# Cross-attention with layer norm in three-pass float32: queries and output tiles as half-row matmuls that share TensorE's rows

## The reference

```python
Q = (x @ w_q.T)      # 16 heads of 32
K = (ctx @ w_k.T); V = (ctx @ w_v.T)
attn = softmax(Q K^T / sqrt(32))      # over 64 keys, per head
o = (attn V) @ w_o.T + b_o
y = layernorm(o + x) * gamma + beta
```

## Time and profile before

| what | value |
|---|---|
| median of 3 runs | 613.66 us (613.42 to 614.11) |
| profiled execution, its own time | 615.86 us |
| its span in the trace | 614.1 us |
| PE busy | 585.9 us (95%) |
| DVE, ACT, POOL busy | 473.2, 444.1, 480.9 us (77%, 72%, 78%) |
| mean granted clock of PE | 0.981 |

### The profile page before, as it was taken

The page is one execution under the profiler, slowest core; times in us unless marked ns, Lnnn a source line. Parts: engine busy times, 40 slices in busy tenths (PEclk is TensorE's granted clock), DMA queues, the critical chain, the costliest instruction groups (busy, mean ns, idle before and its releaser), DMA issues.

```text
span 614.1 us, 8719 instructions
## 1 busy us (share of the span) xinstructions
PE 585.9 (95%) x2602; PEld 425.7 (69%) x2602; DVE 473.2 (77%) x864; ACT 444.1 (72%) x794; POOL 480.9 (78%) x334
## 2 busy tenths in 40 slices
PE   8968789999999999999999999999999999999874
PEld 7745567777777777777777777777777777777553
DVE  7356678888888888888888888888888888888536
ACT  7437777787777877778777787777877778766620
POOL 4336759888898888988889888898888988868740
PEclk9979999999999999999999999999999999999779
DMA  8333413333343334333343233432344321222232
GB/s 311 101 98 85 132 45 98 87 94 113 113 117 86 93 112 118 114 87 91 114 121 115 83 91 115 118 111 86 90 120 117 112 86 50 74 73 74 71 103 86
DMA packets 84223, 63.05 MB, mean 103 GB/s; under 512 B 56752, under 2 KB 56752, under 8 KB 84176
## 3 DMA queue, kind: packets, MB, share of 16 engines
q1 hardware_dynamic: 81936, 62.23, 34.4%
q10 hardware_dynamic: 2240, 0.26, 0.3%
HBM read 39.39 MB, written 16.78 MB: 91 GB/s over the span
## 4 chain that ended last, share of the span: by engine, by line
PE 91%; ACT 2%; DVE 2%; POOL 1%; issue 1%; ACTq 1%; DMA 0%; SPq 0%; DVEq 0%
PE ps_o L280 30%; PE ps_q L280 29%; PE ps_c L280 15%; PE ps_s L334 9%; PE ps_s L344 5%; PE ps_s L280 2%; ACTq L165 1%; ACT probs L476 1%; POOL p_lo L682 1%; PE ps_c L287 1%; DVE z L630 0%; ACT p_hi L409 0%; DMA max_rows<-max_turned 0%; DVE c_raw L605 0%; ACT inverse L483 0%
## 5 line engine op out<-in xcount | busy, mean ns | idle before, releaser
L682 POOL TENSOR_TENSOR p_lo<-probs,p_hi 128x1024 fp32r<-128x1024 f32 x64 | 153.9, 2404 | 53.9 <-ACT p_hi L409 53.9
L576 DVE STREAM_TRANSPOSE turned<-ps_s 128x1024 f32<-128x1024 f32 x64 | 80.0, 1250 | 46.3 <-PE ps_s L334 46.3
L280 PE MATMUL ps_q<-x_hi,wq_lo 128*128 128x512 f32 x256 | 108.7, 425 | 0.0
L280 PE MATMUL ps_o<-wo_hi,c_lo 128*128 128x512 f32 x256 | 104.4, 408 | 2.3 <-POOL c_lo L697 2.3
L470 ACT ACTIVATE inverse<-ps_c 64x512 f32<-64x512 f32 x64 | 38.2, 597 | 89.8 <-PE ps_c L280 89.8
L280 PE MATMUL ps_o<-wo_hi,c_hi 128*128 128x512 f32 x256 | 103.0, 402 | 0.0
L280 PE MATMUL ps_o<-wo_lo,c_hi 128*128 128x512 f32 x256 | 102.9, 402 | 0.0
L280 PE MATMUL ps_q<-x_hi,wq_hi 128*128 128x512 f32 x256 | 102.0, 399 | 0.0
L280 PE MATMUL ps_q<-x_lo,wq_hi 128*128 128x512 f32 x256 | 101.9, 398 | 0.0
L690 POOL TENSOR_TENSOR y<-y,gamma_row 128x512 f32<-128x512 f32 x60 | 77.6, 1293 | 20.4 <-ACT y L512 20.4
L672 POOL TENSOR_TENSOR x_lo<-xT_raw,x_hi 128x512 fp32r<-128x512 f32 x60 | 78.0, 1301 | 18.0 <-ACT x_hi L409 18.0
(11 more groups left out here) (92 smaller groups left out, 1139.4 us busy)
## 6 DMA issues: line engine op xcount, KB each, us to landing
xT_raw<-in_xT SPq DMA_DIRECT2D x64, 256.0 KB, 3.3
x_raw<-in_x SPq DMA_DIRECT2D x64, 256.0 KB, 2.7
out<-y SPq DMA_DIRECT2D x64, 256.0 KB, 2.2
max_rows<-max_turned SPq DMA_DIRECT2D x128, 16.0 KB
ctx_raw<-in_ctxT SPq DMA_DIRECT2D x4, 256.0 KB, 4.2
wk_raw<-in_wkT SPq DMA_DIRECT2D x4, 256.0 KB, 4.4
wq_raw<-in_wqT SPq DMA_DIRECT2D x4, 256.0 KB, 5.9
wv_raw<-in_wvT SPq DMA_DIRECT2D x4, 256.0 KB, 6.8
```

What stands on the lines that cost most here:

```text
L280: mm = nc.tensor.matmul(dst, lhs, rhs, start=(first and n == 0), stop=(last and n == len(passes) - 1))
L576: nc.vector.transpose(turned[:, :], ps_s[:, 2 * s:2 * s + 2, :].rearrange("p b r -> p (b r)")).then_inc(turned_done, 1)
L682: nc.gpsimd.tensor_tensor(p_lo[:, :, :], probs[:, :, :], p_hi[:, :, :].bitcast(fp32), ALU.subtract).then_inc(p_lo_done, 1)
```

## The change

`project_both(n, i, second)` takes the place of `project_queries` and `project_output` in the 56 turns (t = 7 to 62) that have both. Each matmul over 128 rows becomes two over 64 rows. In the first half the queries use rows 0 to 63 and the output tile rows 64 to 127, alternating; then `score(t)` follows; in the second half they change sides, after a wait until the first half's sums have arrived (`first_halves_done`). `combine_values` does the same with the two pairs of heads, in a first and a second part with `subtract_max` and the next tile's bias between them, and comes one turn later. The maxima are read over 64 rows of `select` and `max_rows` (zeros added), and the bias over 64 rows of `signs`. Outputs lag by 7 turns instead of 6, so there is one turn more in all; x is split 5 ahead instead of 6. Buffers are placed anew to make room. The orders on ACT, DVE, POOL and SP are rewritten.

```diff
-    OUT_LAG = 6
-    SPLIT_AHEAD = 6
+    OUT_LAG = 7
+    SPLIT_AHEAD = 5
     LAST = 4
     WARM = 10
...
+                    pe.wait_ge(bias_filled, 16)
                 pe.wait_ge(max_rows_filled, 32 * (n + 1))
                 for pair in range(2):
-                    rows = slice(32 * pair, 32 * pair + 8)
+                    rows = slice(64 * pair, 64 * (pair + 1))
                     mm = nc.tensor.matmul(ps_s[:, 2 * (n % 2) + pair, :], select[rows, :], max_rows[rows, :],
                                           start=False, stop=True, skip_group_check=True)
                 mm.then_inc(shifted_done, 1)
...
                 wait(pe, z_done, i)
-                nc.tensor.matmul(ps_o[:, 0, :], select[64:66, :], max_rows[64:66, :], start=True, stop=False)
+                nc.tensor.matmul(ps_o[:, 0, :], signs[64:128, :, :].rearrange("p a i -> p (a i)"),
+                                 max_rows[64:128, :], start=True, stop=False).then_inc(bias_added, 1)
...
+            def project_both(n, i, second):
...
+                lower, upper = slice(0, 64), slice(64, 128)
+                dims, tile = slice(g * P, (g + 1) * P), slice(t * P, (t + 1) * P)
+                w, x_ = (wq_hi, wq_lo), (x_hi, x_lo)
+                cx, wo = (c_hi[oc % 2], c_lo[oc % 2]), (wo_hi, wo_lo)
+
+                def query(half, k, step):
+                    l, r = ((1, 0), (0, 1), (0, 0))[step]
+                    return nc.tensor.matmul(ps_q[:, 0, :], w[l][half, k, dims], x_[r][half, qc % 2, k, :],
+                                            start=(half is lower and k == 0 and step == 0),
+                                            stop=(half is upper and k == KT - 1 and step == 2))
+
+                def output(half, k, step):
+                    l, r = ((1, 0), (0, 1), (0, 0))[step]
+                    return nc.tensor.matmul(ps_o[:, 0, :], cx[l][half, k, tile], wo[r][half, k, :],
+                                            start=False, stop=(half is lower and k == KT - 1 and step == 2))
+
+                if not second:
+                    wait(pe, q_lo_done, n)
+                    wait_context(i)
+                    for k in range(KT):
+                        if g == 0:
+                            pe.wait_ge(x_lo_done, KT * qc + k + 1)
+                        for step in range(3):
+                            query(lower, k, step)
+                            mm = output(upper, k, step)
+                    mm.then_inc(first_halves_done, 1)
+                else:
+                    pe.wait_ge(first_halves_done, i + 1)
+                    for k in range(KT):
+                        for step in range(3):
+                            mm_q, mm_o = query(upper, k, step), output(lower, k, step)
+                            if k == KT - 1 and step == 2:
+                                mm_q.then_inc(q_product, 1)
+                                mm_o.then_inc(o_product, 1)
+
...
+            def combine_values(n, second):
...
+                for step, (lhs, rhs) in enumerate(((vbd_lo, p_hi), (vbd_hi, p_hi), (vbd_hi, p_lo))):
+                    if not second and step == 2:
+                        pe.wait_ge(p_lo_done, n + 1)
+                    for pair in range(2):
+                        half = 1 - pair if second else pair
+                        rows, cols = slice(64 * half, 64 * (half + 1)), slice(pair * P, (pair + 1) * P)
+                        mm = nc.tensor.matmul(ps_c[:, pair, :], lhs[rows, b % 2, g, cols], rhs[rows, pair, :],
+                                              start=(not second and step == 0), stop=(second and step == 2))
+                mm.then_inc(c_product if second else first_values_done, 1)
 
             project_queries(0)
             project_values(0)
             project_values(1)
             for t in range(SLOTS + OUT_LAG):
-                if t < SLOTS:
+                n, i = t + 1, t - OUT_LAG
+                if n < SLOTS and i >= 0:
+                    project_both(n, i, False)
                     score(t)
-                if 0 <= t - 1 < SLOTS:
-                    subtract_max(t - 1)
-                if t - OUT_LAG >= 0:
-                    start_output(t - OUT_LAG)
-                if t + 1 < SLOTS:
-                    project_queries(t + 1)
+                    project_both(n, i, True)
+                else:
+                    if t < SLOTS:
+                        score(t)
+                    if n < SLOTS:
+                        project_queries(n)
+                    elif i >= 0:
+                        project_output(i)
...
-                if t - OUT_LAG >= 0:
-                    project_output(t - OUT_LAG)
+                if 0 <= t - 2 < SLOTS:
+                    combine_values(t - 2, False)
                 if 0 <= t - 1 < SLOTS:
-                    combine_values(t - 1)
+                    subtract_max(t - 1)
+                if 0 <= i + 1 < TILES:
+                    start_output(i + 1)
+                if 0 <= t - 2 < SLOTS:
+                    combine_values(t - 2, True)
...
             for t in range(SLOTS + OUT_LAG + 2):
-                n = t - 2
+                n = t - 3
...
-                n = t - 1
-                if 0 <= n < SLOTS:
-                    act.wait_ge(shifted_done, n + 1)
-                    wait(act, c_product, n)
-                    nc.scalar.activation(probs[:, :, :], ps_s[:, 2 * (n % 2):2 * (n % 2) + 2, :], ACT.Exp,
-                                         scale=SCALE).then_inc(exp_done, 1)
-                    act.wait_ge(exp_done, n + 1)
-                    to_hi(p_hi[:, :, :], probs[:, :, :]).then_inc(p_hi_done, 1)
+                    act.wait_ge(log_sum_done, n + 1)
+                    nc.scalar.activation(inverse[:, :], inverse[:, :], ACT.Exp, scale=-1.0).then_inc(inverse_done, 1)
                 n = t - 2
                 if 0 <= n < SLOTS:
-                    act.wait_ge(log_sum_done, n + 1)
```

More of the change, by code:

```diff
@@ L52, in cross_attention_kernel @@
             wq_raw, wo_raw, wv_raw = tiled(("wq_raw", "wo_raw", "wv_raw"), fp32, raw)
-        wq_lo, wo_lo, wv_lo = tiled(("wq_lo", "wo_lo", "wv_lo"), fp32r)
+        wq_lo, wo_lo = tiled(("wq_lo", "wo_lo"), fp32r)
+        with ExitStack() as early:
+            wv_lo, = tiled(("wv_lo",), fp32r, early)
+        probs, z = sb("probs", [P, 2, CHUNK], fp32), sb("z", [P, 2, DM], fp32)
         wq_hi, wo_hi = tiled(("wq_hi", "wo_hi"), fp32r)
@@ L78, in cross_attention_kernel @@
         max_rows = sb("max_rows", [P, CHUNK], fp32r)
-        with ExitStack() as raw:
-            probs = sb("probs", [P, 2, CHUNK], fp32, raw)
         p_lo, p_hi = sb("p_lo", [P, 2, CHUNK], fp32r), sb("p_hi", [P, 2, CHUNK], fp32r)
@@ L132, in cross_attention_kernel @@
             sem("max_lo_done"), sem("max_turned_done"), sem("max_rows_filled"))
+        first_halves_done, first_values_done = sem("first_halves_done"), sem("first_values_done")
         shifted_done, exp_done, p_hi_done, p_lo_done = (
@@ L269, in _ @@
                     load_xT(u)
+                if t < SLOTS:
+                    sp.wait_ge(max_turned_done, t + 1)
+                    wait(sp, shifted_done, t)
+                    wait(sp, bias_added, t - OUT_LAG + 2)
+                    for pair in range(2):
+                        sp.dma_start(max_rows[64 * pair:64 * pair + 8, :].bitcast(fp32).rearrange(
+                            "p (b j) -> p b j", j=32), max_turned[:, :]).then_inc(max_rows_filled, 16)
+                i = t - OUT_LAG - 2
+                if i >= 0:
+                    if i < TILES - LAST:
+                        sp.wait_ge(y_done, i + 1)
+                    else:
+                        sp.wait_ge(last_y_done, i - (TILES - LAST) + 1)
+                    sp.dma_start(out[P * i:P * (i + 1), :], y[:, i % 2, :]).then_inc(y_stored[i % 2], 16)
                 next_blocks(t)
@@ L365, in project_output @@
                              first=False).then_inc(o_product, 1)
-            def combine_values(n):
-                b, g = n // PER_BATCH, n % G
-                pe.wait_ge(p_lo_done, n + 1)
-                wait(pe, c_raw_done, n)
-                if n == 0:
-                    pe.wait_ge(values_lo_done, 3)
-                if n % PER_BATCH == 0:
-                    pe.wait_ge(vbd_filled[b % 2], 16 * 16 * (b // 2 + 1))
-                for pair in range(2):
-                    cols = slice(pair * P, (pair + 1) * P)
-                    mm = three_passes(ps_c[:, pair, :], [((vbd_hi[:, b % 2, g, cols], vbd_lo[:, b % 2, g, cols]),
-                                                          (p_hi[:, pair, :], p_lo[:, pair, :]))])
-                mm.then_inc(c_product, 1)
+            def project_both(n, i, second):
+                qc, g = divmod(n, G)
+                oc, t = divmod(i, G)
+                lower, upper = slice(0, 64), slice(64, 128)
[13 more added lines that the diff above has]
+                    wait(pe, q_lo_done, n)
+                    wait_context(i)
```

(34 more changed lines are left out.)

163 lines of the change are left out of this document (78 added, 85 removed).

## The result

The kernel after takes 636.16 us (median of 4 runs, 634.54 to 638.18) beside 613.88 for the one before (4 runs, 613.42 to 616.00): 1.0358 times as long, with an interval of 1.0315 to 1.0400. It is slower, as forecast, but 11.4 us more so than the 624.8 of the forecast, and just above the upper end of its range, 636. (It was one of the quicker runs; the medians lie 22.3 apart.)

A forecast was written before the change was run, and what follows sets the result against it. PE was taken to bound the kernel before at 8.53 us a slot, a DVE-ACT ring of 8.65 us the one after. Middle +6.8, end +4.3 and start 0 on 613.66 gave 624.8 us, range 606 to 636.

The forecast's parts named there:

- The new ring: Closed ring of 14 instructions on DVE and ACT, gone round once a turn whatever PE does: 8.65 us.
- past `shift` to `half_max`: Ring step on DVE from `turned` over `shift` to the large `half_max`, with overlaps of 0.08: 1.30 us.
- "the second" `c_raw`: Ring step on DVE from the first `c_raw` to the second: 0.65 us.
- End +4.3: End of the kernel: one more output tile still to be done, at the last tiles' distance of 4.28 us.
- Start 0 +- 2: First turns: 0.31 more in some four turns, set equal to slot 2's score no longer waiting for slot 0's values.
- The change on PE: PE in a turn: 35 steps of 0.23 run through in 8.05 us, instead of 8.53.
- alone this would save 0.48 us: PE's shorter turn by itself, if the other engines follow: 0.48 us in each of 56 turns, 27 us.
- Rival 2: Ring on DVE and ACT: nothing overlaps, 9.05 us a turn, 647 us; chance 0.08.
- Rival 1: Handovers overlap throughout, ring 8.33, 607 us; without a binding ring PE's 8.05, 591; together 0.22, 0.04 for 591.
- Rival 3: Half-row pairs on PE take 0.26 us a step, 9.1 us a turn, 650 us; chance 0.05.
- rival 4: The change does nothing that counts: ring at 8.45, time within 0.2%; chance 0.05.
- four steps of the ring read PSUM: Remark that the skill's warning, tiling doesn't speed up the evacuation of PSUM, agrees with the main case.

The follow-up runs named there:

- e1_swap: The kernel after with two ACT instructions exchanged, `probs` ahead of `max_hi`: 604.73 us, 0.9849 of the kernel before.
- e7_best: The kernel after with the edits of e1_swap and e6_vhi, and on DVE the small `half_max` ahead of `z`: 604.69 us, 0.9843 of the kernel before.
- e2_shift: The kernel after with `shift` behind the large `half_max` on DVE and `y` behind `q_hi` on ACT: 636.94 us, ratio 1.0364 to the kernel before.
- e3_light: The kernel after without the low-part matmuls of three of four k tiles in queries and outputs, 23 PE steps a turn instead of 35: 638.05 us, one run.
- e4_lag7: The kernel before with OUT_LAG = 7 instead of 6 and nothing else: 614.61 us, ratio 1.0012.
- e6_vhi: The kernel after with the fourth value tile's `values_hi` in turn 1 moved behind `q_hi` on ACT: 633.14 us, ratio 1.0302 to the kernel before.
- e11_bias: e7_best with the next tile's bias matmul on PE behind the second part of the values: 595.87 us, 0.9693 of the kernel before.

## Why the prediction was right in direction and short in size

**"The new ring" was right.** All 14 instructions are there in the predicted order, with waits only at `c_raw` and `max_hi`, and e1_swap, which cuts the ring at one place, takes the time away. Step by step, in the order of the prediction, the trace has 0.61, 0.23, 0.14, 1.03, 0.61, 0.62, 0.67, 0.69, 0.72, 1.42, 1.12, 0.72, 0.21; the forecast was 0.61, 0.25, 0.12, 1.04, 0.61, 0.62, 0.66, 0.65, 0.72, 1.30, 1.14, 0.72, 0.21. The assumption that a change of partitions allows no overlap held in each place where the sum uses it, but it was put too broadly. All these places have the upper half on one side. Between the lower half and all partitions the overlap stays: the row maximum starts at 300.06 while `q_lo` ends at 300.14, `bn_stats` at 300.18 while the row maximum ends at 300.26, and the sum's own `max_hi` to `probs` is such a pair. e7_best moves one such border: `z` behind the small `half_max`, which reads the upper half, starts 0.04 us after its end (306.89 + 0.18 to 307.11), and `q_lo` behind `z` 0.07 before (307.11 + 0.69 to 307.73).

Of the 11.4 us by which the forecast fell short, 7.7 are the ring, in two mis-sized terms, and 4.5 the start; the end took 4.2 off again. The rest, 3.4 us, is that the profiled run of the kernel after lies below its median and that of the kernel before above it.

**Mis-sized: "past `shift` to `half_max`", 1.25 - 0.08 + 0.21 - 0.08 = 1.30.** It measured 1.42. `shift` starts 0.04 us after the end of `turned`, on which it doesn't depend. I took the overlap of 0.08 from an instruction ahead of this transpose; behind it there is none. 302.66 + 1.25 to 303.95 is 0.04 too, and I put that down to dependence. e2_shift shows that both followers start 0.04 behind the transpose. Why `shift` does stays open. It may be the transpose. It may also be the halves again: `shift` reads SBUF at partition 0, and the last instruction that read SBUF ahead of it was the second `c_raw`, at partition 64 (`turned` reads PSUM). For the second speaks that the small transpose `max_turned` is overlapped by 0.07 us in the kernel before (306.68 + 0.21 to 306.82). No run parts the two.

**Mis-sized: "the second" `c_raw`, 0.65.** It measured 0.69, since the first one takes 0.68 us instead of 0.64. Before, it overlapped the end of `max_turned`; now it comes after a wait. e3_light, where PE has much less to do, has 0.68 too, so PE's load isn't the cause; why it is longer after a wait stays open. Together the two terms are +0.16, the others -0.02: 8.79 instead of 8.65, and 56 x 0.14 = 7.8 us.

**"End +4.3" failed.** It measured +0.1, and why is known only in part. I took the earlier trace rows, one tile every 4.28 us, for the price of each tile still to be done. But how many tiles follow one another at the end is set by the values of the last slot, not by the lag. The chain in order of time, in the kernel after:

```profile
607.69 0.70 DVE c_raw L647
...
610.99 3.02 PE ps_o L285 x12
...
623.82 3.02 PE ps_o L285 x12
```

The last `c_raw` ends at 608.39, and from 610.99 to 623.82 four tiles start, 4.28 us apart. Before, too, four tiles follow the last `c_lo`, the last of them at 604.69, and in both 9.38 us lie from there to the span's end. The tile that the lag adds is done while PE waits for that slot anyway; e4_lag7 has it at 1.9 us, and the end scatters by as much between the kernels here (46.1 to 49.0 us). But the clock has a part in it. The kernel before, one stretch of its end (its third number from the end, 0.64, is the granted clock) and two tiles of its chain:

```profile
574.99:582.99 8.00, 8.00 (x24) 5.57 (x22) 3.07 (x6) 5.82 (x11) 5.87 (x5) 0.64 0.28 85
```
```profile
575.16 5.42 PE ps_o L280 x12
589.63 5.25 PE ps_o L280 x12
```

PE had waited 2.25 us ahead of each of them (or of the values just before), and nearly all of both ran at 1.2 GHz: 10.67 us instead of 2 x 3.02, so 4.6 us more. e4_lag7 has one such tile (5.43 us), the kernel after none on its chain. An estimate from these rows: at an equal, full clock the end before would be up to 4.6 us shorter, which would put the difference near the forecast's 4.3. Against this, the medians of e4_lag7 and the kernel before differ by 0.2 us, with 0.8 saved at the start (8.53 - 7.71). What the lag costs at an equal clock stays open.

**"Start 0 +- 2" failed.** It measured +4.5. The ring without `shift` and `z` was right, 8.07 us a turn from slot 3 to 6 (8.18 to slot 7) where I had 8.03. What I hadn't looked at is which one-off work stands in ACT's queue in the turns 1 and 2 now that their order is new: `values_hi` ahead of `q_hi`, 3.5 us by e6_vhi. End and start together were +4.6 beside a forecast of +4.3, by chance.

**"The change on PE" was right for the kernel after:** steps of 0.23 (0.234), 35 of them, and PE not the bound. At 0.234 the 35 steps are 8.19 us, not 8.05, and its "alone this would save 0.48 us" a turn is more than any version here got: 0.21 with the ring cut (e1_swap), 0.28 with the bias moved (e11_bias). The result asked for at `z` is there at 306.35 + 0.39 = 306.74, 0.57 us ahead of 307.31, where I had 0.4 of slack. Nothing lengthened the ring from there, as e3_light shows. One of its sums doesn't come out: what the earlier trace rows leave of the slot is 8.53 - 6.55 = 1.98 us, not 1.64. The forecast doesn't use it.

**The rivals.** Rival 2, no overlap at all, 647 us (by its own terms, 0.45 instead of 0.4 more, it would be 9.10 and 650), is not the mechanism: `q_lo` to the maximum, `max_hi` to `probs`, `shift` to `half_max` and `half_max` to `z` overlap by about 0.08 to 0.09 us each. The section of the Trainium skill that the prediction drew on for it, "The DRAIN you can't avoid" of "VectorE: DVE Perf Modes", goes on to say that a next operation that is not held starts earlier. With this second sentence the trace agrees: of these four, the three on DVE started 0.08 to 0.09 us early. Rival 1's PE bound at 8.05 isn't reached by any version: e1_swap has 8.32, e11_bias 8.25. Rival 3, slow pairs, is refuted by 0.234, and rival 4, no difference, by the 3.6%. The remark that four steps of the ring read PSUM is a miscount: `q_lo`, `probs`, both `Ln`, both `c_raw`, `turned` and `z` are eight of the 14.

## What to carry to other kernels

When an edit takes work off the engine that is the bound, write down the closed rings of the new queues (each instruction that waits for another engine, and what is queued behind it there) and add up their lengths before counting the gain: here a `probs` queued behind `max_hi` turned a gain of 0.2 us a turn into a loss of 0.26. Then look for the cheapest place to cut the ring, which can be an exchange of two instructions on an engine that is 70% busy. And read the overlap of two neighbours from rows with the same instructions and the same halves of the partitions ahead, since it depends on that.
